# Transformer block with routed experts on one core: ScalarE rounds the expert weight chunks of the shared-expert pass, ScalarE and VectorE split the last two, and the row-name loads come in growing groups

## What is computed

```python
logits = x @ gate_w.T;  scores = softmax(logits)
topk_w, topk_i = top_k(scores, 2)               # of 8 experts
topk_w = topk_w / topk_w.sum(-1) * 2.5
y   = sum over the chosen e of topk_w * (silu(x @ w_gate[e]) * (x @ w_up[e])) @ w_down[e]     # 256 -> 352 -> 256
out = x1 + layernorm(y + (silu(x @ sw_gate) * (x @ sw_up)) @ sw_down)                         # shared: 256 -> 704 -> 256
```

## Time and profile before

| | us |
|---|---|
| median of 3 runs | 1858.62 (1854.68 to 1861.70) |
| time of the profiled execution | 1857.21 |
| its span | 1855.3 |
| TensorE busy | 1740.7 (94%) |
| VectorE busy | 1259.0 (68%) |
| ScalarE busy | 992.1 (53%) |
| GpSimd busy | 932.3 (50%) |

### The profile page before, as it was taken

How to read it: one execution, slowest core, us unless ns; L and a number is a source line. 1 busy time by engine, 2 the same in 40 slices (tenths; PEclk the granted TensorE clock), 3 DMA queues, 4 the chain that set the end, 5 groups by cost and what they waited for, 6 DMA issues and landing times.

```text
span 1855.3 us, 39544 instructions
## 1 busy us (share of the span) xinstructions
PE 1740.7 (94%) x13060; PEld 1425.3 (77%) x13060; DVE 1259.0 (68%) x3077; ACT 992.1 (53%) x2309; POOL 932.3 (50%) x1117
## 2 busy tenths in 40 slices
PE   4999999999999999997999998999999999989996
PEld 3566666666666666655888887999999999978886
DVE  7778888888888888785776775433333333358787
ACT  2566666777777667666333333444444444435554
POOL 3445555555555555554378766455555555401101
PEclk8999999999999999998999999999999999999999
DMA  6655556655565665443254322233222222257875
GB/s 120 100 74 92 103 102 127 115 98 102 103 101 100 109 115 104 92 91 120 92 113 89 90 42 57 70 76 87 75 75 75 75 75 76 71 191 184 204 210 97
DMA packets 164113, 189.78 MB, mean 102 GB/s; under 512 B 41777, under 2 KB 121970, under 8 KB 163922
## 3 DMA queue, kind: packets, MB, share of 16 engines
q1 hardware_dynamic: 136642, 142.92, 36.9%
q0 software_dynamic: 24976, 43.41, 9.4%
q10 hardware_dynamic: 2304, 0.93, 0.3%
HBM read 84.87 MB, written 51.40 MB: 73 GB/s over the span
## 4 chain that ended last, share of the span: by engine, by line
PE 69%; DVE 8%; ACT 7%; issue 6%; POOL 5%; SPq 3%; DMA 1%; ACTq 1%; POOLq 0%; DVEq 0%
PE bank L496 5%; PE bank L497 5%; PE bank L498 5%; PE bank L1636 5%; PE bank L2485 4%; PE bank L2486 4%; PE bank L2484 4%; PE bank L1693 4%; PE bank L1658 4%; PE bank L1638 3%; ACT prob L1074 3%; PE bank L1637 3%; PE bank L2505 2%; PE bank L2506 2%; PE bank L2507 2%
## 5 line engine op out<-in xcount | busy, mean ns | idle before, releaser
L924 POOL TENSOR_SCALAR_AFFINE_SELECT prob<-prob 128x512 f32<-128x512 f32 x256 | 162.9, 636 | 380.3 <-ACT prob L1074 380.2
L1074 ACT ACTIVATE prob<-bank 128x512 f32<-128x512 f32 (+1 forms) x512 | 249.0, 539 | 103.4 <-PE bank L1680 100.8
L2376 DVE TENSOR_TENSOR b_h<-b_h,bank 128x352 f32<-128x352 f32 x135 | 70.4, 521 | 287.3 <-ACT b_h L2330 287.3
L2306 POOL DMA_INDIRECT y_scratch<-b_y,names x135 | 133.6, 989 | 176.4 <-ACT b_y L2341 172.4
L1399 DVE COPY_PREDICATED bank<-from_prev,bank 128x512 f32<-128x512 int32 x192 | 133.1, 693 | 96.2 <-PE bank L1658 92.0
L1402 DVE TENSOR_REDUCE row_max<-bank 128x4 f32<-128x512 f32 x256 | 177.3, 693 | 25.8 <-PE bank L1658 18.5
L2484 PE MATMUL bank<-wgu_h,bxT_h 128*128 x540 | 176.5, 327 | 0.0
L2485 PE MATMUL bank<-wgu_l,bxT_h 128*128 x540 | 176.2, 326 | 0.0
L2330 ACT ACTIVATE b_h<-bank 128x352 f32<-128x352 f32 x135 | 62.7, 464 | 211.9 <-PE bank L2486 211.9
L2486 PE MATMUL bank<-wgu_h,bxT_l 128*128 x540 | 175.3, 325 | 0.0
L2300 POOL DMA_INDIRECT bx<-xn_scratch,names x135 | 134.6, 997 | 54.6 <-issue 39.2
(11 more groups left out here) (359 smaller groups left out, 5247.5 us busy)
## 6 DMA issues: line engine op xcount, KB each, us to landing
kS<-qk_h SPq DMA_DIRECT2D x128, 128.0 KB, 3.9
qS<-qk_h SPq DMA_DIRECT2D x128, 128.0 KB, 5.8
f_y<-y_scratch SPq DMA_DIRECT2D x16, 1024.0 KB, 9.2
x_in<-in_L_attn_x_dram SPq DMA_DIRECT2D x16, 512.0 KB, 6.2
kS<-qk_l SPq DMA_DIRECT2D x64, 128.0 KB, 4.8
qS<-qk_l SPq DMA_DIRECT2D x64, 128.0 KB, 6.6
x_res<-in_L_attn_x_dram SPq DMA_DIRECT2D x16, 512.0 KB, 4.1
out_dram<-x_res SPq DMA_DIRECT2D x16, 512.0 KB, 5.1
```

The lines of the kernel that those rows point to most:

```text
L924: op = e.affine_select(out=own, in_=own, compare_op=ALU.is_gt, fill=0.0, base=0, pattern=[[0, HG], [1, P]], channel_multiplier=-1)
L1074: e.activation(prob[:, u % SLOTS, 2 * hp:2 * hp + 2, 0:w], src[:, :, 0:w], ACT.Exp, scale=SCALE).then_inc(keyed.frees[hp], 1)
```

## The change

The chunks' rounding from chunk 2 on goes from GpSimd's queue to ScalarE's, at fixed places: in step m (1 to 6) chunk 2m after n = 1 and chunk 2m + 1 after n = 4; in step 7 chunks 14 and 15 after n = 1 and n = 2. GpSimd keeps the subtraction for chunks up to 13; VectorE takes it for 14 and 15. The exponentials of the routing move from behind the pass into step 7, after n = 3, and the small Silu behind them is dropped. ScalarE now rounds all three pieces of the down weights, and VectorE subtracts them, the second after the rows of blocks 0 and 1, the third after its step 0 of the second pass. The useless matmuls go from 18 to 14. `b_h` changes places in memory with `bhT_h` and `bhT_l`, so the wait for the stored result of step 7 moves from `gate` to `hidden_turned`.

```diff
-                        gp.wait_ge(stage_in, 32 * (CHUNKS if k >= CHUNKS - 2 else k + 1))
-                        e.tensor_copy(hi, chunk_of(k)).then_inc(chunk_high, 1)
+                        hi, lo = parts_of(k)
+                        if k < 2:
+                            gp.wait_ge(stage_in, 32 * (k + 1))
+                            e.tensor_copy(hi, chunk_of(k)).then_inc(chunk_high, 1)
                         gp.wait_ge(chunk_high, k + 1)
                         e.tensor_tensor(lo, chunk_of(k), hi.bitcast(f32), ALU.subtract).then_inc(stage_split, 1)
...
-                    for k in (CHUNKS - 2, CHUNKS - 1):
-                        split_chunk(k)
...
+                    def chunk_rounded(k):
+                        act.wait_ge(stage_in, 32 * (CHUNKS if k >= CHUNKS - 2 else k + 1))
+                        act.wait_ge(stage_split, min(k, CHUNKS - 2))
+                        nc.scalar.activation(parts_of(k)[0], chunk_of(k), ACT.Copy).then_inc(chunk_high, 1)
...
+                            if m == HALF - 1:
+                                if n in (1, 2):
+                                    chunk_rounded(CHUNKS - 3 + n)
+                                if n == 3:
+                                    exponentials()
+                            elif m > 0 and n in (1, 4):
+                                chunk_rounded(2 * m + (n == 4))
...
-            GROUPS = [range(0, 1), range(1, 2), range(2, 4), range(4, 16), range(16, 56), range(56, NBLK)]
+            GROUPS = [range(0, 1), range(1, 2), range(2, 4), range(4, 8), range(8, 16), range(16, 32), range(32, 64), range(64, NBLK)]
...
                     act.wait_ge(down_in, 16 * FCE)
+                    act.wait_ge(table_ready, 1)
+                    down_rounded(0)
+                    act.wait_ge(h_used, FCS * HALF)
+                    for n in range(2):
+                        shared_result(act, HALF - 1, n, lambda n: y_sb[:, 2 * n:2 * n + 2, :].rearrange("p t d -> p (t d)"))
+                    act.wait_ge(stage_split, CHUNKS)
+                    down_rounded(1)
                     act.wait_ge(hl_ready, FCS * HALF)
-                    e.activation(wd_h[0:fe[LATE], LATE, :, :], wd_f[0:fe[LATE], LATE, :, :], ACT.Copy).then_inc(down_high, 1)
+                    down_rounded(2)
...
+                    down_remainder(0)
                     rows_low(0, 0)
                     rows_low(1, 1)
+                    down_remainder(1)
...
                         step(b, b % 2)
+                        if b == 0:
+                            down_remainder(2)
...
-                    for _ in range(18):
+                    for _ in range(14):
```

More of the change, by code:

```diff
@@ L143, in sandwich_kernel @@
     SETUP_STEPS, NORM_STEPS, TAIL_STEPS, RESIDUAL_STEPS = 19, 2, 5, 4
-    ROUTE_STEPS, END_STEPS, WEIGHT_STEPS, LAST_STEPS = 20, 8, 12, 17
+    ROUTE_STEPS, END_STEPS, WEIGHT_STEPS, LAST_STEPS = 20, 8, 10, 17
     xn2_dram = nc.dram_tensor("xn2_scratch", (SEQS, S, D), f32, kind="Internal").ap()
@@ L234, in sandwich_kernel @@
         reserve("gate_and_up", words(wgu_h, wgu_l))
-        b_h = sb("b_h", [P, 2, F])
         bhT_h = sb("bhT_h", [P, 2, FCE, P], f32r)
         bhT_l = sb("bhT_l", [P, 2, FCE, P], f32r)
+        b_h = sb("b_h", [P, 2, F])
         phase.close()
@@ L1978, in chunk_of, with parts_of @@
                     return chunk_in[:, :] if k < CHUNKS - 1 else arena[:, LAST_CHUNK:LAST_CHUNK + 2 * F]
+                def parts_of(k):
+                    return tuple(w[:, k, :, :].rearrange("p k f -> p (k f)") for w in (wgu_h, wgu_l))
                 def store_result(sp, m):
@@ L2028, in split_chunk @@
                     def split_chunk(k):
-                        hi, lo = (w[:, k, :, :].rearrange("p k f -> p (k f)") for w in (wgu_h, wgu_l))
-                        gp.wait_ge(stage_in, 32 * (CHUNKS if k >= CHUNKS - 2 else k + 1))
-                        e.tensor_copy(hi, chunk_of(k)).then_inc(chunk_high, 1)
+                        hi, lo = parts_of(k)
+                        if k < 2:
+                            gp.wait_ge(stage_in, 32 * (k + 1))
+                            e.tensor_copy(hi, chunk_of(k)).then_inc(chunk_high, 1)
                         gp.wait_ge(chunk_high, k + 1)
@@ L2059, in result, with exponentials @@
                             shared_result(act, m, n, lambda n: y_sb[:, 2 * n:2 * n + 2, :].rearrange("p t d -> p (t d)"))
+                    def chunk_rounded(k):
+                        act.wait_ge(stage_in, 32 * (CHUNKS if k >= CHUNKS - 2 else k + 1))
+                        act.wait_ge(stage_split, min(k, CHUNKS - 2))
+                        nc.scalar.activation(parts_of(k)[0], chunk_of(k), ACT.Copy).then_inc(chunk_high, 1)
+                    def exponentials():
+                        act.wait_ge(member_ready, 2 * HALF)
+                        nc.scalar.activation(probs, lg_all[:, :, :], ACT.Exp).then_inc(exp_ready, 1)
                     for m in range(HALF):
@@ L2067, in _ @@
                                 first_chunk(act, m, n)
+                            if m == HALF - 1:
[5 more added lines that the diff above has]
+                                chunk_rounded(2 * m + (n == 4))
                         if m + 1 < HALF:
                             gate_silu(act, m + 1, 0, h_f)
-                    result(HALF - 1)
                 @block.vector
@@ L2099, in experts_reached, with last_chunk_low @@
                         e.tensor_tensor(row_end, spare_end, row_start, ALU.subtract).then_inc(blocks_known, 1)
+                    def last_chunk_low(k):
+                        dve.wait_ge(chunk_high, k + 1)
+                        hi, lo = parts_of(k)
+                        e.tensor_tensor(lo, chunk_of(k), hi.bitcast(f32), ALU.subtract).then_inc(stage_split, 1)
                     def finish_table():
@@ L2122, in last_step @@
                         experts_reached()
+                        last_chunk_low(CHUNKS - 2)
                         hidden(dve, m, 3, h_f)
                         hidden_low(dve, m, 3, h_f, h_h, h_l)
+                        last_chunk_low(CHUNKS - 1)
                         finish_table()
@@ L2250, in sandwich_kernel @@
                 REST = F - FULL * P
-                LATE = FCE - 1
                 def lists_written(eng):
@@ L2326, in gate @@
                     def gate(b, u):
-                        if isinstance(b, int) and b == 0:
-                            act.wait_ge(ys_stored, 16 * HALF)
                         act.wait_ge(bg_full, b + 1)
@@ L2332, in hidden_turned @@
                     def hidden_turned(b, u):
+                        if b == 0:
+                            act.wait_ge(ys_stored, 16 * HALF)
                         act.wait_ge(bt_full, b + 1)
@@ L2341, in result, with down_rounded @@
                         e.activation(b_y[:, u, :], psum[5][:, 0:D], ACT.Copy).then_inc(by_read, 1)
+                    def down_rounded(n):
+                        e.activation(wd_h[0:fe[n], n, :, :], wd_f[0:fe[n], n, :, :], ACT.Copy).then_inc(down_high, 1)
                     act.wait_ge(down_in, 16 * FCE)
+                    act.wait_ge(table_ready, 1)
[5 more added lines that the diff above has]
+                    down_rounded(1)
                     act.wait_ge(hl_ready, FCS * HALF)
-                    e.activation(wd_h[0:fe[LATE], LATE, :, :], wd_f[0:fe[LATE], LATE, :, :], ACT.Copy).then_inc(down_high, 1)
+                    down_rounded(2)
                     rows_high(0, 0)
@@ L2395, in link, with down_remainder @@
                         dve.wait_ge(s, value)
-                    dve.wait_ge(down_in, 16 * FCE)
-                    for n in range(LATE):
+                    def down_remainder(n):
+                        dve.wait_ge(down_high, n + 1)
                         hi, lo, raw_ = down_part(n)
-                        if n == 1:
-                            dve.wait_ge(stage_split, CHUNKS)
-                        link(e.tensor_copy(hi, raw_))
                         e.tensor_tensor(lo, raw_, hi.bitcast(f32), ALU.subtract).then_inc(down_low, 1)
+                    down_remainder(0)
                     rows_low(0, 0)
                     rows_low(1, 1)
-                    dve.wait_ge(down_high, 1)
-                    hi, lo, raw_ = down_part(LATE)
-                    e.tensor_tensor(lo, raw_, hi.bitcast(f32), ALU.subtract).then_inc(down_low, 1)
+                    down_remainder(1)
                     def step(b, u):
```

3 lines of the change are left out of this document (removed).

## The result

| | before | changed |
|---|---|---|
| median of 16 runs each, us | 1858.01 (1850.71 to 1865.91) | 1865.86 (1861.42 to 1872.91) |
| ratio, 95% interval | | 1.0043 (1.0029 to 1.0057) |
| profiled execution, its span, us | 1857.21, 1855.3 | 1869.11, 1867.4 |

A forecast was written before the change was run, and what follows sets the result against it. TensorE, busy nearly all the time, was taken as the bound, so only its gaps and low-clock stretches could give time back. Transition -1.0 and name groups -5.0 made -6.0 us: 1852 from the median 1858.6, range 1846 to 1859.

The forecast's parts named there:

- The twelve roundings in steps 1 to 6: First pass: ScalarE's added roundings, 0.76 us each, fit its idle time or delay `rows_high` by 0.1; counted at nothing.
- ScalarE late: Rival, chance 0.05: if a rounding took over 2.5 us, twelve would cost 1.3 us each or more; 1868 and more.
- The clock holds: Rival, chance 0.13: three mid-pass stretches of lower TensorE clock, 1.7 us each, go or come; with them gone, 1847.
- Name groups: Second pass, block 16: smaller groups of name loads remove TensorE's wait for rows and the cold clock after it, -5.0 us.
- List writes: End of first pass: GpSimd waits for ScalarE at every chunk, so the last list write begins 2.6 us later.
- First gathers: Start of second pass: gathers no longer behind a chunk, 0.96 us each instead of 2.90 and 2.73; -4.3 us.
- long gathers: Rival, chance 0.17: the first gathers after the lists keep taking 2.90 and 2.73 us; 1856.
- list writes slip further: Rival, chance 0.17: chunk 13 also waits for its load, so the transition eats the groups' gain; five more us give 1858.
- Down remainders: Second pass, before block 2: TensorE waits about 0.9 us for VectorE's third piece, 0.22 replacing an earlier wait; +0.7 us.
- the transition: From first to second pass: rows of block 1 come 1.7 us earlier, less 0.7 for the down remainders; -1.0 us.

The follow-up runs named there:

- E5: Changed kernel with GpSimd also rounding chunks 2 and 3, and ScalarE's second rounding of a step after n = 5 instead of n = 4: 1856.10 us, ratio 1.0005.
- E6: Changed kernel with GpSimd also rounding chunks 2 and 3, ScalarE from chunk 4 on, still after n = 1 and n = 4: 1858.05 us, ratio 1.0020.
- E4: Changed kernel with GpSimd rounding every chunk but the last two again: 1850.05 us, ratio 0.9955; repeated in another set: 1847.17 us, ratio 0.9946.
- E2: Kernel before the change with only the new name groups (1, 1, 2, 4, 8, 16, 32, 71): 1854.76 us, ratio 0.9978.
- E3: Changed kernel with the old name groups (12, 40, 79 behind the first four blocks): 1870.91 us, ratio 1.0076.
- E9: E4 with VectorE's down remainders 0 and 1 ahead of the rows of blocks 0 and 1, and 2 right behind them: 1847.74 us, ratio 0.9967.
- E10: E9 with 25 useless matmuls at the transition instead of 14: 1848.29 us, ratio 0.9946.

## Why the prediction was wrong

- **The step that failed** is "The twelve roundings in steps 1 to 6 ... At nothing". I priced each by its 0.76 us against ScalarE's idle time before its next instruction, read in step 6, where chunks are early. In step 1 the instruction also waits for its operand: 17.29 us, +15.0 us for the step. I had written the rule ("each microsecond would reach `gate_up` of the next step") but gave ScalarE no wait for a load there. The rival "ScalarE late" had the side right and the cause wrong: no rounding is long.
- **A second fault of the same step** is its size in the other steps. "Delays `rows_high` by 0.1, and TensorE is still busy with logits" fell: against an undisturbed step a rounding at n = 4 costs 0.9 us (E5 against E6), of which 0.7 shows as TensorE's wait for `rT_l`. Step 6, where I had read the idle times, hid it: TensorE waits there 0.66 us for VectorE's `rt` before the change, and the step takes 31.45 us before and 31.54 after. Nor did it show in the sum of steps 2 to 6: in the profile of before, steps 2 to 5 take 123.17 us, 4.9 over four times the undisturbed 29.57, with a granted clock of 0.95 in two of them and 0.5 us of waiting for `rt` in two; those of after take 122.65, 0.7 over four times 30.49, with 0.95 in one. Whether that difference belongs to the change stays open; in E4's two profiles the same excess was 3.3 and 6.4 us, so it varies between executions of one kernel. That leaves the rival "The clock holds" unsettled, and no run shows that it is the phase of the work that decides when the clock falls.
- **Name groups, -5.0:** -5.3 in the spans, 4.1 in E2, 6 in E3, the last two with wide intervals. Right. No later group was late.
- **List writes, +2.6:** +2.1. Near enough, with some luck: 24 writes from 1099.6 at the 1.31 us of its own rows end in one at 1129.7, which is +3.1. E4 shows that the middle roundings alone cause the delay.
- **First gathers, -4.3:** right, 1.00 and 0.96 us; the rivals "long gathers" and "list writes slip further" fell. The forecast chose between 0.96 and 2.90 us by VectorE's rows, and that choice held; E9 and E10 show the cause, the remainder that lies on a gather. Whether its two SBUF inputs are what does it, no run varied.
- **Down remainders, +0.7, and the transition, -1.0 in all:** 1.01 us of waiting and -1.21.
- **What stays open:** E4 and E6 differ by 0.65% of ratio, 12 us, and by the two intervals 7 to 17. Steps 2 to 5 with 0.9 each, 2.6 for chunk 4 and 1.95 in the transition (43.26 against 41.31) make 8.2; the rest is not accounted for.

Without the middle roundings the forecast's other terms, -6.0 without the +2.6 of the list writes, give -8.6; E4 measured -8.4 (0.9955) and -10.0 (0.9946 in the repeat).

## What to carry to other kernels

When an instruction moves to an engine that is in the critical loop, price the wait for its operand at every place where it stands, the first above all: find in the old trace when the operand is there (here 941.87) and when the engine passes the place (924.8), and count what is queued behind. An engine that runs 17 us late off the critical path looks free; the one that takes over a link of its chain inherits the whole lateness. Where two things hold the same wait, as chunk 1's load and GpSimd's eight writes did here, relieving one gives at most what it was longer by. And a wait read from one execution varies: 17.29 and 16.30 us for the same first pass.

## What the hardware showed beside it

VectorE and GpSimd can hold each other up for a whole instruction. Two pairs in the changed kernel, GpSimd's gathers of blocks 4 and 6 (shown above) and VectorE's remainders beside them:

```profile
1160.90 2.28 DVE L2432 TENSOR_TENSOR wd_l<-wd_l,wd_h 128x2048 fp32r<-128x2048 f32 x1
...
1165.06 2.28 DVE L2432 TENSOR_TENSOR wd_l<-wd_l,wd_h 96x2048 fp32r<-96x2048 f32 x1
```

The gathers begin 0.24 and 0.49 us after a remainder and end 0.82 and 0.81 us after it ends, whatever their start (E9's 0.84 after); a free one takes 0.95. The other way round, a small step of the routing on VectorE (line 662), which has a median of 0.19 us, begins in the same instant as GpSimd's subtraction and ends with it. The line's instructions (shortest, median and longest in ns), the long one, and GpSimd beside it, in the changed kernel:

```profile
L662 DVE SCALAR_TENSOR_TENSOR rt<-rt x16: 191/192/1747, 875.4 to 1126.9; 128x32 f32<-128x32 f32 x16
```

```profile
1084.88 1.74 DVE L662 SCALAR_TENSOR_TENSOR rt<-rt 128x32 f32<-128x32 f32 x1
```

```profile
1084.87 1.71 POOL L2038 TENSOR_TENSOR wgu_l<-chunk_in,wgu_h 128x704 fp32r<-128x704 f32 x1 [3.34 <-ACT wgu_h L2067]
```

Not every instruction is held: VectorE's product at 1100.61, with one input in PSUM, keeps its 0.69 us inside GpSimd's subtraction of 1099.51 to 1101.55. Nor does a gather that begins first hold up a remainder: the first gather of E9 begins at 1129.98, the remainder at 1130.07, and they take 1.00 and 2.29 us.

The Trainium skill (SBUF — State Buffer, "SBUF: two separate sides") calls the pair of ports that VectorE and GpSimd share an exclusive lock: of a GpSimd instruction and one of VectorE of certain kinds, one with two SBUF inputs among them, the first to start holds it for its whole instruction. The rows of the two pairs and of line 662 agree; E9's first gather does not show it.
